# Leaving out the products that nobody reads, in a twelve-stage decoder kernel

## What is computed

```python
x = x + attn(_layernorm(x))
x = x + xattn(_layernorm(x), ctx_768)
x = x + ffn(_layernorm(x))
```

## Time and profile before

| | |
|---|---|
| median of 3 runs | 1397.62 us (1390.81 to 1398.3) |
| the profiled execution | 1394.62 us |
| its span | 1392.8 us |
| mean granted clock of TensorE in it | 0.984 of full |
| TensorE busy | 1299.6 us, 93% |
| VectorE, ScalarE, GpSimd busy | 929.3, 670.7, 344.7 us |

### The profile page before, as it was taken

How to read it: one execution, slowest core, us unless ns; L and a number is a source line. 1 busy time by engine, 2 the same in 40 slices (tenths; PEclk the granted TensorE clock), 3 DMA queues, 4 the chain that set the end, 5 groups by cost and what they waited for, 6 DMA issues and landing times. The chain is left out here.

```text
span 1392.8 us, 28874 instructions
## 1 busy us (share of the span) xinstructions
PE 1299.6 (93%) x11350; PEld 824.5 (59%) x11350; DVE 929.3 (67%) x1885; ACT 670.7 (48%) x1694; POOL 344.7 (25%) x373
## 2 busy tenths in 40 slices
PE   8999999999999899989989889999989999999986
PEld 6766555445666675667768567844445555654333
DVE  6786766435676565357674378688887876778655
ACT  5886533333677554345212247235557677730002
POOL 4000330001111100014121020377784664400001
PEclk9999999999999999999999999999999999999999
DMA  4000104110000000000204020101101111799980
GB/s 138 3 2 2 41 0 188 57 45 16 2 2 3 2 18 0 22 2 3 111 38 137 12 90 3 47 16 46 46 31 21 28 18 20 177 216 256 247 191 16
DMA packets 25350, 80.50 MB, mean 58 GB/s; under 512 B 5371, under 2 KB 7306, under 8 KB 24834
## 3 DMA queue, kind: packets, MB, share of 16 engines
q1 hardware_dynamic: 24354, 75.53, 20.1%
q10 hardware_dynamic: 864, 3.15, 0.8%
HBM read 72.11 MB, written 1.08 MB: 53 GB/s over the span
## 5 line engine op out<-in xcount | busy, mean ns | idle before, releaser
L187 POOL TENSOR_TENSOR rstd<-var,minus_half 128x4 f32<-128x4 f32 x30 | 31.2, 1040 | 541.4 <-DVE var L144 514.8
L575 DVE TENSOR_REDUCE quad_max<-psum 128x1 f32<-128x128 f32 (+3 forms) x256 | 113.1, 483 | 54.0 <-PE psum L436 51.9
L530 ACT ACTIVATE pt<-psum,quad_max 128x128 f32<-128x128 f32 (+3 forms) x256 | 133.3, 530 | 26.7 <-DVE quad_max L575 26.6
L196 PE MATMUL psum<-ident 128*128 128x128 f32 x996 | 123.8, 282 | 9.2 <-DMA ident<-in_ident 3.9
L196 PEld LDWEIGHTS psum<-ident 128*128 128x128 f32 x996 | 118.0, 196 | 15.8 <-issue 6.0
L3025 PE MATMUL psum<-pt,slots 128*128 128x512 f32 x256 | 114.7, 599 | 6.2 <-DVE pt L3180 6.0
L3004 PE MATMUL psum<-slots,xn_t 128*128 128x512 f32 x256 | 112.6, 600 | 3.1 <-DVEq L3151 3.1
L2762 ACT ACTIVATE p<-psum,duo_max 128x512 f32<-128x512 f32 x128 | 86.8, 683 | 42.7 <-DVE duo_max L2797 42.6
L3095 ACT ACTIVATE pt<-psum,p 128x64 f32<-128x64 f32 x256 | 57.8, 392 | 71.4 <-POOL wide L3237 43.7
L3025 PEld LDWEIGHTS psum<-pt,slots 128*128 128x128 f32 x256 | 47.0, 189 | 73.0 <-issue 47.7
L2797 DVE TENSOR_REDUCE duo_max<-psum 128x1 f32<-128x512 f32 x128 | 82.3, 684 | 10.4 <-PE psum L2673 8.3
(11 more groups left out here) (516 smaller groups left out, 2795.2 us busy)
## 6 DMA issues: line engine op xcount, KB each, us to landing
pt<-scratch_out_gates SPq DMA_DIRECT2D x32, 256.0 KB, 13.3
heads<-scratch_out_gates SPq DMA_DIRECT2D x24, 256.0 KB, 15.8
slots<-in_s_l0f SPq DMA_DIRECT2D x8, 514.0 KB, 3.3
wide<-scratch_gates SPq DMA_DIRECT2D x8, 512.0 KB, 7.7
slots<-in_s_l3v SPq DMA_DIRECT2D x8, 512.0 KB, 3.3
context_v<-scratch_out_gates SPq DMA_DIRECT2D x16, 256.0 KB, 18.2
slots<-in_s_l3o ACTq DMA_DIRECT2D x6, 512.0 KB, 10.4
weights<-in_w_l1a SPq DMA_DIRECT2D x1, 2624.0 KB, 9.4
```

Source lines behind the costliest of these rows:

```text
L196: nc.tensor.matmul(m.ps[bank][:, 0:P], m.ident[:, :], m.ident[:, :], start=True, stop=True, skip_group_check=True)
L530: nc.scalar.activation(m.quad_p[:, i % 2, g, 0:keys], m.ps[g][:, 0:keys], ACT.Exp, bias=m.quad_max[:, i % 2, g:g + 1], accum_out=sum_colum ...
L575: nc.vector.tensor_reduce(m.quad_max[:, n % 2, g:g + 1], m.ps[g][:, 0:keys], AX.X, ALU.max, negate=True).then_inc(m.quad_negmax, 1)
```

## The change

`keep_busy` does nothing any more. All its calls stay, so TensorE waits for the same semaphores, with nothing issued between them, and every other instruction of every engine stays and keeps its order.

```diff
@@ -191,9 +191,7 @@
 def keep_busy(nc, m, n, bank=IDLE_BANK):
-
-    for _ in range(n):
-        nc.tensor.matmul(m.ps[bank][:, 0:P], m.ident[:, :], m.ident[:, :], start=True, stop=True, skip_group_check=True)
+    pass
```

## The result

| | before | after |
|---|---|---|
| median of 16 runs each | 1397.80 us (1390.81 to 1401.61) | 1412.38 us (1402.38 to 1421.49) |
| ratio | | 1.0116, 95% interval 1.0094 to 1.0138 |
| the profiled execution, its span | 1394.62, 1392.8 us | 1411.61, 1409.8 us |
| mean granted clock of TensorE in it | 0.984 | 0.932 |

The changed kernel is slower by 1.2%, 14.6 us between the medians and 17.0 us between the two profiled executions. Ratios leave out executions that lie far above the rest of their kernel; what those are is the subject of the last experiment.

The account below looks back on a forecast made before the run. TensorE, busy 93%, was taken to set the pace inside most stages and wait between them; 1394.6 us plus 18.2 for the low clock less 4.0 of holding gave 1409 us, range 1397 to 1424.

Parts of the forecast that it names:

- The sum: Whole change: +18.2 us for low clock behind waits, -4.0 us for held time given back, +14.2 us in all.
- The forecast's case: Whole kernel slower, about 1409 us (1401 to 1418), stage starts moving apart 1 to 2 us at each norm; chance 0.58.
- Part 1: All waits: removing products that only fill a wait gains nothing, since the next step starts when its input is done.
- Part 2: Starts of l1a, l1x, l2x, l3x: products hold TensorE past its input; removal gives -4.0 us, bounds 0 and -6.0.
- Part 3: Behind long waits and at two first-step places: work restarts at the low clock, +18.2 us, bounds 0 and +42.
- the count of places: Nine long waits plus three counted half: 10.5 low-clock spells of 3.4 us, costing 1.45 us each, 15.2 us.
- a second spell: Behind a wait: another 3.4 us at low clock follows because work does not lift it; upper bound 3.4 us lost.
- B: Rival, whole kernel: held time is given back and the clock costs nothing, -6.0 us, 1389 us; chance 0.07.
- A': Rival, stage starts: most low-clock spells hidden, only half on the path, +9.1 with -4.0, 1400 us; chance 0.23.
- C: Rival, l2x, l3x and l1a's start: clock stays low through attention, about +25 us on top, 1434 us; chance 0.12.

Follow-up runs that it names:

- the last experiment: Kernel before without l2x's and l3x's first-step products (line 1989) alone, twelve runs: near group ratio 0.9944, far group 25.4 us above it by the means.
- half as many narrow products: Kernel before with its unread products on 32 x 32 of the array instead of 128 x 128, and half as many: 1418.4 us, ratio 1.0169.

## Why the prediction was right

**The sum** was +14.2 us; +14.6 was measured between the medians and +17.0 between the profiled executions. The forecast's case came in, at a step a stage, and 1409 us lies 3.4 us under the median. The parts were less exact than the sum.

**Part 1, the products are worth nothing by themselves:** held. Outside the stretch of streamed weights every step down of more than 1 us in the changed kernel is at an attention's first steps.

**Part 2, the holding, -4.0 us:** right in mechanism and place, too small. In the account of the changed kernel the steps down are -3.2 us at l1a, -1.3 at l1x, -3.4 at l2x (5.5 to 2.0 by 637 us, before a low spell at 640.0 takes 1.6 back) and -2.1 at l3x, -10.0 in all, beyond my bound of -6.0. As a gain in time it is less: the kernel without these calls alone shows -4.6 us by the ratio (-0.3 to -9.1), with the higher ones of its executions in it, and of the -8.9 between the profiled executions some 3 are spells of the kernel before. Two steps failed. In l1a I took 1.1 us from the first call alone and left out the two in the loop; in l2x I took VectorE's idle time before the third scores for the whole, 1.8 us, though the calls of 6, 4, 3 and 3 hold the later scores as well. And the factor of two thirds, because the scores would run at the low clock, cut what was too small already: in l2x the third scores last 0.79 us in the rows of the changed kernel (at 633.65), as at full clock.

**Part 3, the clock, +18.2 us:** the mechanism was right and the count of places nearly so, the length was not. With -10.0 of steps down, a whole of +17.0 leaves +27 of steps up in the profiled execution, which I put down to the clock; by ratios the norms cost 13.7 us where the count had 10.2, and the tables 4.9 where I had 4.4. Behind two waits the low level lasts 9 and 17 us of work instead of 3.4 (before l0f, at the end of l2x), and those places cost 3.6 us (4.8 in the kernel without the norms' products) and 3.1 us instead of 1.5. I had a second spell as the upper bound and gave it no place. The gates of l3f, left out for having a spell already, cost 1.1 us; the +1.1 at the norm before l3a, left out for the same reason, is no more than four kernels that keep that norm's products have there (+0.7 to +1.1). Before 712.8 us the kernel before has such a spell as well, and there I did count one. The spell of 1.5 us that I put at l1a did not show: both kernels have the same low stretch of 6.8 us there (from 341.9 before, 346.4 after); +0.8 was predicted, -3.2 measured. So both terms were too small in this execution, by 6 and by 9 us, and the sum came out because they stand against each other. That it did so within 3 us is luck.

**The rivals.** B, faster, is refuted: it needs part 3 under a third of 18.2 us, and the norms alone cost 13.7. A', half hidden, is refuted for the sum; single steps are as small as that. The Trainium skill (TensorE: Matmul & The Clock Gate, What's actually happening) puts the loss of getting the clock up under 1% of a span. Measured here is 1.16% net, with the gain of part 2 in it, and 0.98% from the norms alone; for a kernel of twelve stages, each with waits, the figure is no bound. C, the clock low through attention, is not in the trace of the changed kernel, whose l2x is back at 1.00 by 650 us. The same page (Part 4: PE-mode transpose) has it that transposes do not bring the clock up; the stretch from 650 to 660 us, with transposes in each step, stands at 1.00, as it did before the change. So they did not keep the clock down here; whether they would bring it up by themselves the trace can't say, since 63 transposes stand among 144 other products in it. But something of C's kind may exist: a kernel with only line 1989's products gone has 25 us more in six executions of twelve, with the clock to match.

**Open:** where the far executions lose their 23 to 25 us (no trace of one was taken), whether the spread of the changed kernel, 1402 to 1421 us, is the same thing in smaller pieces, and what of the 7 us between the changed kernel and half as many narrow products is holding; and what sets how long the clock stays low behind a wait, 3.4 us at one place and 17 at another.

## What to carry to other kernels

A wait of a tuned kernel can be paid for twice, once as idle time and again as slow work behind it: price a removed filler by the work that runs at the low clock behind each wait and is waited for, not by the time at the low level, half of which lay in the waits here. Fill the waits in which nothing is due, and stop before the input arrives; in a stage's first steps a count sized by the trace (5, 3, 1, 4, 2, 2 instead of 16, 4, 6, 4, 3, 3) gave the lowest times here, but with one far execution of six, while the full count had none of eight. And where two kernels issue the same instructions on one engine, lay their starts side by side: it turns one difference of 17 us into thirteen. Do the same for two executions with the same instructions, to see how large a step must be to count.

## What the runs showed of the hardware that was not expected

- Products on 32 x 32 of the array keep TensorE busy (95%) and do not keep its clock up (0.928; with none 0.932). At the low level one starts 213 ns after the other instead of 109, and the kernel with them is 82 us slower.
- 147 us more at the low level cost 15 to 17 us; in half of them TensorE had nothing to do.
- After a restart the clock can stay low for 9.2 us with TensorE busy without a break, and for 17.1 us with it busy 15.0 of them.
- A program on one core can have two sets of executions, 25 us apart, with mean clocks of 0.957 to 0.963 and 0.979 to 0.984, and which of them comes is not settled by the program; with 56 products in the first steps of two stages the slower one came in none of 70 executions.
